# Normalising the mixer's output with tokens on partitions, and issuing the last sequence's tail in the second phase

## The reference, cut to what matters

```python
n  = layernorm(x) * (1 + scale_a) + shift_a
xs, z = split(n @ W_in.T)                 # 512 channels each
B, C  = xs @ W_B.T, xs @ W_C.T            # 16 states each
dt = softplus(xs @ W_dt.T + b_dt)
h[t] = exp(dt[t]*A) * h[t-1] + dt[t]*B[t]*xs[t]      # per channel and state
y[t] = sum_over_states(h[t]*C[t]) + D*xs[t]
x1 = x + gate_a * ((y * silu(z)) @ W_out.T)
h2 = layernorm(x1) * (1 + scale_b) + shift_b         # over the 256 features
out = x1 + gate_b * two_layers(h2)                   # attention (window 128), gated MLP
```

## Time and profile before

| what | us |
|---|---|
| three runs: median (lowest to highest) | 4182.83 (4182.79 to 4183.98) |
| the profiled execution | 4186.23 |
| its span, first to last instruction | 4184.4 |
| set-up and the first sequence's head, until the first x load of the loop after it | 0 to 55 |
| from the first to the last-but-one x1 store of phase one (14 passes) | 195.0 to 1646.2 |
| phase one's last store | 1751.0 |
| phase two: first store of layer 0, last store of layer 0 | 1953.2, 3037.7 |
| first and last store of the output | 3117.0, 4181.1 |

### The profile page before, as it was taken

One profiled execution on the slowest core, in us unless ns is written; L12 is line 12 of the kernel. 1 busy time (PEld: TensorE's weight loads), 2 busy tenths in 40 slices (PEclk: granted clock), 3 DMA queues, 4 the chain that ended last, 5 costly groups with the idle time before them and its releaser, 6 DMA issues.

```text
span 4184.4 us, 61077 instructions
## 1 busy us (share of the span) xinstructions
PE 3982.3 (95%) x19870; PEld 2670.8 (64%) x19870; DVE 3624.9 (87%) x6114; ACT 2743.5 (66%) x5896; POOL 2670.3 (64%) x1298
## 2 busy tenths in 40 slices
PE   7999999999999999769999999999999999999997
PEld 4444444444444444347887778787777878777785
DVE  5999999999999999768888888877888887878884
ACT  6677777777777775336767676666767666666764
POOL 3999999999999999553434444443534444343442
PEclk8999999999999999879999999999999999999998
DMA  3333333333333333420000000001110101000010
GB/s 109 117 124 124 122 122 121 122 121 121 122 122 123 125 122 116 137 91 27 21 26 17 31 16 31 16 31 51 36 63 21 41 21 37 26 31 32 21 36 26
DMA packets 119610, 295.11 MB, mean 71 GB/s; under 512 B 21288, under 2 KB 45664, under 8 KB 119296
## 3 DMA queue, kind: packets, MB, share of 16 engines
q1 hardware_dynamic: 117424, 291.15, 21.1%
q10 hardware_dynamic: 1872, 0.05, 0.0%
HBM read 248.52 MB, written 42.64 MB: 70 GB/s over the span
## 4 chain that ended last, share of the span: by engine, by line
PE 51%; DVE 2%; ACT 1%; DMA 1%; issue 1%; POOL 1%; SPq 0%; DVEq 0%; ACTq 0%; POOLq 0%
PE b_bank L1346 12%; PE b_bank L1474 12%; PE b_bank L1495 6%; PE b_bank L1425 5%; PE b_bank L1398 5%; PE b_bank L1409 5%; PE b_bank L1439 4%; PE b_bank L1378 3%; DMA b_hx<-stack_rows 1%; PE b_bank L1446 1%; ACT b_probs_t L1586 0%; DVE b_hx_part L1728 0%; DVE b_qk_rot L1773 0%; PE b_bank L1510 0%; POOL b_scores L1704 0%
## 5 line engine op out<-in xcount | busy, mean ns | idle before, releaser
L824 POOL TENSOR_TENSOR a_state<-a_state,a_c_wide 128x1024 f32<-128x1024 f32 x512 | 1195.1, 2371 | 19.7 <-DVE a_state L766 19.7
L1704 POOL TENSOR_TENSOR b_scores<-b_scores,b_row_rate 128x1024 f32<-128x1024 f32 (+1 forms) x256 | 458.2, 1801 | 825.6 <-DVE b_row_rate L1825 825.6
L584 PE MATMUL a_y_sum<-a_state,a_ident 128*128 128x512 f32 x2048 | 951.2, 597 | 6.8 <-POOL a_state L824 6.8
L766 DVE TENSOR_TENSOR_SCAN a_state<-a_decay,a_slot 128x1024 f32<-128x1024 f32 x352 | 788.7, 2270 | 0.7
L1346 PE MATMUL b_bank<-b_w_qkv,b_hx_part 128*128 128x512 f32 x2304 | 604.8, 408 | 29.9 <-DVE b_hx_part L1728 9.1
L584 PEld LDWEIGHTS a_y_sum<-a_state,a_ident 128*128 128x128 f32 x2048 | 387.3, 191 | 383.0 <-issue 316.7
L1677 POOL TENSOR_TENSOR b_by_cos<-b_qk,b_rotary 128x1024 f32<-128x1024 f32 x128 | 310.2, 2424 | 475.5 <-DVE b_qk L1757 473.4
L1474 PE MATMUL b_bank<-b_hn_part,b_w 128*128 128x512 f32 x2112 | 526.2, 399 | 7.0 <-DVE b_hn_part L1728 6.9
L695 ACT ACTIVATE a_decay<-a_dt,a_neg_a 128x512 f32<-128x512 f32 x704 | 453.8, 710 | 114.5 <-DVE a_state L766 114.1
L1574 ACT ACTIVATE b_scores<-b_scores,b_row_bias 128x256 f32<-128x256 f32 (+1 forms) x1024 | 478.2, 472 | 69.4 <-DVE b_row_bias L1814 69.4
L1346 PEld LDWEIGHTS b_bank<-b_w_qkv,b_hx_part 128*128 128x128 f32 x2304 | 428.3, 192 | 128.8 <-issue 16.4
(11 more groups left out here) (211 smaller groups left out, 6946.2 us busy)
## 6 DMA issues: line engine op xcount, KB each, us to landing
a_c_wide<-bc_rows SPq DMA_DIRECT2D x256, 512.0 KB, 3.8
a_b_wide<-bc_rows SPq DMA_DIRECT2D x80, 512.0 KB, 4.8
b_hx<-stack_rows SPq DMA_DIRECT2D x64, 256.0 KB, 3.9
b_x_res<-stack_rows SPq DMA_DIRECT2D x32, 512.0 KB, 3.4
a_xt<-in_L_attn_x SPq DMA_DIRECT2D x16, 512.0 KB, 5.4
x_rows<-a_x_t SPq DMA_DIRECT2D x16, 512.0 KB, 5.4
stack_rows<-a_h_t SPq DMA_DIRECT2D x16, 512.0 KB, 5.3
stack_rows<-b_xc SPq DMA_DIRECT2D x16, 512.0 KB, 2.9
```

The lines of the kernel that those rows point to most:

```text
L584: last = nc.tensor.matmul(y_sum[dd][:], ident[:], state[state_ring.slot[q]][:, i, :], start=False, stop=(j == GROUPS - 1 and i == GROUP - 1))
L766: nc.vector.tensor_tensor_scan(flat(h), flat(factor), flat(term), 0.0, ALU.mult, ALU.add).then_inc(scan_done.sem, 1)
L824: nc.gpsimd.tensor_tensor(h[:], h[:], c_wide[c_ring.slot[q // 2]][:], ALU.mult).then_inc(cmul_done.sem, 1)
L1704: nc.gpsimd.tensor_tensor(probs, probs, row_rate[:, w, at].unsqueeze(2).to_broadcast([P, 4, hi - lo]), ALU.mult)\
```

## The change: what it does

Seven things are changed together.

1. The tail's normalisation has tokens on partitions. `turn2` (PE, 8 transposes of x1), `tot2` (ACT copies 4 tiles of 128x256 out of PSUM with a row sum), `stat2` (ACT: mean, 4 squares with a row sum, Ln, Exp), `norm2` (ACT: 4 shifts of 128x1 and 4 scalings of 128x256), `hT2` (PE, 8 transposes back) and `h2` (ACT modulates from PSUM). `mean2`, `cen2`, `sq2`, `var2`, `dev2` and `xn2` go.
2. B and C go through the spreading matmul as two F32R parts on 64 rows. `bcrest` and `bcmid` go.
3. Unit 9's `mul` goes from POOL to DVE (`TO_VECTOR = 9`), with a `bcast` of its own.
4. The one-column cut of dt goes from POOL (L807) to ACT (`cut`).
5. The tail of sequence 15 leaves phase one: its steps are issued by each engine inside `FIRST_ORDER` of phase two, so phase one's block ends with the last gate. Banks 6 and 7 are free for phase two when its `h2` is done.
6. SP in phase two: `load_first` comes ahead of the first pass and holds layer 0's weights and the three early spares. The later spares, `w_o` and the vectors (`load_rest`) stay behind phase one's last stores, after `h2store:0` in the first pass. At the change of layer, the q and k weights are asked for as soon as the last projection that used them is done, and `w_1` and `w_2` two passes later in `load_hx`, after the rows.
7. `MIXER_ORDER`, `ORDER`, `BANK_OF` and `FIRST_ORDER` are all new. The head's `norm` writes in place and waits for the transposes of x, and sequence 0's `norm` moves from the set-up to the loop. In the set-up one load goes and `picks` is F32.

```diff
-    1: "xload xT xcopy stat norm hT mod up hcut xs xscopy bc bccopy cstore bcup bcrest bcmid bclow dt soft dtadd"
-       " z zcopy silu",
+    1: "xload xT xcopy stat norm hT mod up hcut xs xscopy bc bccopy cstore bcup bclow dt soft dtadd"
+       " z zcopy silu cut",
     0: "skip bcast cload bload decay mul scan cmul sum gate",
-    -1: "out res x1store mean2 cen2 sq2 var2 dev2 xn2 h2 h2store"}
+    -1: "out res x1store turn2 tot2 stat2 norm2 hT2 h2 h2store"}
+TAIL_STEPS = MIXER_STEPS[-1].split()
...
-        by_pool = [q for q in units if q // 2 in POOL_LOADS]
+        by_pool = [q for q in units if q // 2 in POOL_LOADS and q != TO_VECTOR]
...
-                    last = nc.tensor.matmul(slots[q % 2][:, i, :], picks[0:96, GROUP * j + i, :], bc_parts[slot][0:96, :],
+                    last = nc.tensor.matmul(slots[q % 2][:, i, :], picks[:, GROUP * j + i, :].bitcast(F32R), bc_parts[slot][:].bitcast(F32R),
                                             start=True, stop=True)
...
+            def copy_tail(s, slot, i):
+                wait(act, h2_turned, s - 1, CHUNKS)
+                wait(act, x1_turned, s, i + 1)
+                for t in (2 * i, 2 * i + 1):
+                    at = (t % 2) * DIM
+                    nc.scalar.activation(xn2[t], bank(f"turn2{i}")[:, at:at + DIM], ACT.Copy, accum_out=neg_mean2[:, t:t + 1])\
+                        .then_inc(total2_done.sem, 1)
...
 FIRST_ORDER = """
-pss:0 pnorm:0 prot:0 padd:0 pq:0 pk:0 v:0 pss:1 psq:0 prate:0 vc:0 psq:1 prate:1 ptc:0 pnorm:1 pk:1 prot:1 vc:1 vc:2
-psq:2 prate:2 v:1 pq:1 padd:1 hxs:0 pss:2 pnorm:2 v:2 ptr:0 prot:2 padd:2 pk:2 ptc:1 pq:2 psq:3 hxload:0 pq:3 pss:3
-pnorm:3 prot:3 ptr:1 padd:3 pk:3 ptc:2 prate:3 ptc:3 ptr:2 mask:0.0 mask:0.1
+out:0 pq:0 pk:0 res:0 psq:0 pss:0 prate:0 pnorm:0 out:1 v:0 res:1 x1store:0 vc:0 prot:0 turn2:0 turn2:1 tot2:0
+tot2:1 pk:1 pq:1 psq:1 padd:0 pss:1 prate:1 pnorm:1 v:1 stat2:0 vc:1 prot:1 padd:1 ptr:0 pq:2 pk:2 psq:2 pss:2 ptc:0
+v:2 prate:2 pnorm:2 norm2:0 vc:2 prot:2 ptr:1 padd:2 hT2:0 hT2:1 h2:0 h2:1 h2store:0 hxload:0 pk:3 pq:3 psq:3 pss:3
+ptc:1 prate:3 hxs:0 pnorm:3 ptr:2 ptc:2 v:3 vc:3 prot:3 padd:3 ptc:3 pn:0.0 pn:0.1
 """
...
                 if s == BATCH:
                     for done, group in zip(moved, (early, late)):
                         sp.wait_ge(done, 3 * loads_of(group))
-                    load_qkv()
+                    sp.wait_ge(q_full.sem, q_full.at(s - 1, TILES))
+                    load_qkv(0)
+                    sp.wait_ge(k_full.sem, k_full.at(s - 1, TILES))
+                    load_qkv(1)
+                    sp.wait_ge(v_done.sem, v_done.at(s))
+                    load_qkv(2)
```

More of the change, by code:

```diff
@@ L116, in host_constants @@
     pick = np.zeros((P, STATES), np.float32)
-    for part in range(3):
+    for part in range(2):
         pick[2 * STATES * part + np.arange(STATES), np.arange(STATES)] = 1.0
@@ L161 @@
[L161 to L165, removed]
@@ L497, in _ @@
                           "h2store": store_h2})
+            for signal, per_pass in ((xs_full, INNER_CHUNKS), (z_full, INNER_CHUNKS), (bc_full, 1), (dt_full, INNER_CHUNKS)):
+                wait(sp, signal, BATCH - 1, per_pass)
+            wait(sp, h2_stored, 0, 1)
+            first.load(sp)
+            first.tail["SP"] = {"x1store": store_x1, "h2store": store_h2}
         @block.tensor
@@ L718, in _ @@
-                           "bcmid": middle_bc, "decay": decays, "sq2": square_tail, "dev2": deviation_tail, "h2": modulate_tail})
+                           "xscopy": copy_x, "zcopy": copy_z, "silu": silu, "soft": softplus, "cut": cut, "bccopy": copy_bc, "bcup": upper_bc,
+                           "decay": decays, "tot2": copy_tail, "stat2": statistics_tail, "norm2": normalise_tail, "h2": modulate_tail})
+            first.tail["ACT"] = {"tot2": copy_tail, "stat2": statistics_tail, "norm2": normalise_tail, "h2": modulate_tail}
@@ L804, in add_parts @@
                     .then_inc(u_done.sem, 1)
-                wait(pool, u_done, s, half + 1)
-                nc.gpsimd.tensor_tensor(dt[slot][:, pair, 0:1], half_cut[:], half_cut[:], ALU.add).then_inc(dt_done.sem, 1)
             def scan_input(s, slot, q):
@@ L840 @@
 ORDER = """
-ptr-:3 v-:3 hxs:0 mask:1.0 vc-:3 mask:1.1 score:0.0 score:0.1 score:1.0 hxload:0 exp:0 rate:0 add:0 pss:0 score:1.1
-wo:0 psq:0 pk:0 x1load:0 pq:0 add:1 exp:1 rate:1 wo:1 v:0 pnorm:0 prate:0 v:1 pt:0.0 pn:0.0 pn:0.1 pt:0.1 vc:0 mean:0
-score:2.0 pt:1.0 cen:0 pn:1.0 mask:2.0 resload:0 pt:1.1 pn:1.1 store:0 sq:0 pt:1.2 pt:1.3 prot:0 psq:1 vc:1 pq:1 sqs:0
-pss:1 padd:0 xn:0 mask:2.1 pk:1 dev:0 v:2 prate:1 vc:2 var:0 ptc:0 hns:0 hn:0 pnorm:1 att:0 mask:3.0 score:2.1 onorm:0
-onorm:1 prot:1 rate:2 padd:1 gated:0 ptr:0 pn:2.0 gated:1 hl:0 pss:2 outstore:0 exp:2 mask:3.1 gelu:0 gelu:1 psq:2
@@ new lines @@
+exp:1 wo:0 pq:0 pk:0 mask:1.1 wo:1 pn:1.0 rate:0 add:0 pt:0.0 pss:0 prate:0 x1load:0 add:1 rate:1 v:0 pt:0.1 mask:2.0
+pnorm:0 pn:1.1 score:2.0 cen:0 score:2.1 mean:0 v:1 mask:2.1 prot:0 sq:0 pt:1.0 pk:1 psq:1 sqs:0 pt:1.1 resload:0 vc:0
+pq:1 pss:1 pt:1.2 padd:0 pnorm:1 dev:0 prate:1 vc:1 xn:0 outstore:0 ptc:0 v:2 pt:1.3 vc:2 onorm:0 hns:0 hn:0 var:0
+mask:3.0 pk:2 att:0 ptr:0 mask:3.1 prot:1 rate:2 pn:2.0 padd:1 pq:2 hl:0 score:3.0 gated:0 pn:2.1 score:3.1 exp:2
+gelu:0 psq:2 gated:1 hl:1 gelu:1 pss:2 onorm:1 hh:0 att:1 hh:1 gelu:2 ga:0 hl:2 gated:2 prate:2 ptc:1 ga:1 pnorm:2
@@ L851 @@
+pn:3.0 ga:2 prot:2 ptr:1 exp:3 rate:3 gated:3 hh:2 ga:3 pt:2.0 ga:4 pt:2.1 wd:0 gelu:3 hl:3 gated:4 pt:2.2 wd:1 ga:5
+gelu:4 hh:3 pq:3 hl:4 pk:3 gated:5 wd:2 ptr:2 padd:2 pss:3 hl:5 wd:3 pn:3.1 hh:4 gelu:5 psq:3 pnorm:3 ptc:2 pt:2.3
+wd:4 hh:5 store:0 fin:0 prate:3 pt:3.0 wd:5 fin:1 pt:3.1 sum:0 pt:3.2 prot:3 turnc:0 sum:1 padd:3 turnc:1 pt:3.3 vc:3
+ptc:3 pn+:0.0 v:3 att:2 turn:0 turn:1 pn+:0.1 onorm:2
 """
 BANK_OF = """
-q_t3:5 k_t3:1 wo0:5 s0_0_0:6 s0_0_1:0 s0_1_0:4 s0_1_1:5 wo1:7 s1_0_0:2 s1_0_1:3 q0:4 k0:1 s1_1_0:0 s1_1_1:6 pt0_0:3
```

332 lines of the change are left out of this document (172 added, 160 removed).

## The result

The changed kernel takes 4218.2 us (median of 4 runs, 4217.2 to 4218.9) against 4182.8 for the kernel before on the same chip: ratio 1.0085, 95% interval 1.0068 to 1.0103. It is 0.85% slower, where -44 us were forecast. Its profiled execution took 4217.7, with a span of 4215.8.

What follows compares the result with a forecast made beforehand. DVE was taken to bound phase one, PE phase two and a chain the seam. Terms -28 + 2 - 9 - 7.5 - 2 = -44.5 us gave 4141.7 from the profiled 4186.2, stated as 4139; own range 4124 to 4152, wider 4118 to 4166.

Steps and rivals of the forecast that it cites:

- Phase one, a pass: Phase one's passes: DVE binds and loses 1.72 us a pass, 103.66 to 101.94; PE needs 97.6 to 101.5; term -28.
- PE or ACT takes over: Rival for phase one: PE reaches 103.3 us a pass, the term is -8 in place of -28, 4159 us; chance 0.14.
- The first gate: Prologue: sequence 0's norm moves into the loop, a shorter cut of B and C offsets part; +2 us (0 to +6).
- The last pass: Last pass of phase one: has no head, is set by POOL with one mul fewer; -2 us.
- if the 0.34 of idle stay: Phase one: condition that DVE's idle 0.34 us a pass remains, for a pass to become 101.94.
- The clock: Phase one: by the skill's rule on transposes, PE's new 2.4 us could cost 2.4 more; weighed with the PE rival.
- The seam: Between phases: the block ends with the gate, 18.5 us sooner, but SP's queue gives back 10.2; taken as -9.
- the seam gives nearly all: Rival: h2 is early or the first attention pass gets shorter, 10 us more won, 4129 us; chance 0.13.
- The change of layer: Phase two's 80.20 us pass: q and k weights asked for earlier remove PE's wait behind queued loads; -7.5 us.
- the moved loads: Phase two: earlier q and k loads give -7.5 us, w_1 and w_2 no longer ahead of a rows load give -2.
- The rest of phase two: Other phase-two passes: PE is full, so the new order can't take much off 71.7; 0, bounds -0.3 and +2 a pass.
- the bound of -5 for phase one: Phase one's term of -28: its weak end, -5 us, if PE or ACT takes over.

Runs made afterwards that it cites:

- E6: The changed kernel with its F32R spreading matmuls on 96 rows instead of 64, the added rows zero; 4125.0 us.
- E4: The kernel before with only phase two's new ORDER, BANK_OF and FIRST_ORDER, without the tail's steps; 4134.3 us.
- E7: The kernel before with phase two's new order and also the moved loads of layer 1's weights; 4134.5 us.
- E11: The changed kernel with F32R spreading on 96 rows, and DVE's gates multiplying only 64 of 512 columns; 4112.2 us.

## Why the prediction was wrong

**The step that failed** is PE's price in "Phase one, a pass": "its spreading matmuls go from 44 at BF16 to 46 at F32R", put at -1.0 to +2.9 us. I priced the form from `dt`'s row of 128 rows and let the rows go from 96 to 64 without a term. The form was priced rightly for 96 rows: PE needs 100.3 a pass there, inside my 97.6 to 101.5. The rows cost 0.39 us a unit, 9 us a pass; with them PE is busy 106.7 of a pass of 109.2, and DVE waits for it. The rival "PE or ACT takes over" named the engine, but its upper end, 103.3, was built on the same price.

**Phase one's own gain** would have been missed too. E6 stands 4 us behind before at the last gate, not 26 ahead. The first gate comes 5 us later (131.7 against 126.6, where I said +2; E4 and E7, with before's own set-up, show 129.6 and 126.7, so 3 of the 5 can be scatter). DVE loses 1.0 of busy time a pass and not 1.7, a third of that is lost in waits among three engines, and 0.6 us a pass goes to the clock. The last pass, said to give 2, gave nothing. "if the 0.34 of idle stay" was the weak clause. POOL was taken as no bound once unit 9 had moved, and it is none (100.3 busy); without that move a pass would be 105.4.

**The clock.** The Trainium skill's page "TensorE: Matmul & The Clock Gate", part 4, says that transposes don't count as work that keeps the clock up; I weighed it as 2.4 us more a pass. After's five passes with 32 transposes each average 1.00, with one short fall among them (the windows show 0.82, 0.50 and 0.83 from 666 to 672 us), so that price is not seen. What the runs do show is a clock that falls at a stretch of waits, and holds when ordinary matmuls take the place of the waiting.

**The seam** held. After's queue of SP shows sequence 1's rows asked for at 1894.96, which is +68.0 from the last gate's end (1826.94), where +69.5 was counted; the spare stores come directly behind the loads, as said:

```profile
1868.26 0.34 SPq L507 DMA_DIRECT2D stack_rows<-a_h_t  x1
...
1884.64 1.62 SPq L1296 DMA_DIRECT2D b_w_whole<-in_L_ffn_w  x2
1886.30 5.69 SPq L1289 DMA_DIRECT2D w_part<-b_probs_t  x6
1892.03 2.88 SPq L1289 DMA_DIRECT2D w_part<-b_scores  x4
1894.96 1.09 SPq L1313 DMA_DIRECT2D b_hx<-stack_rows  x2
```

With phase two's order equal (E6 against E7), gate to first store is 202.7 against 214.1: -11.4 for -9. The other 7 us come with phase two's new order (before against E7), as the rival "the seam gives nearly all" had it. Together they are 19, over the 15 that was to count as wrong.

**The change of layer** was right in size and wrong in cause. The pass of 80.20 became 71.2, but E4 has 70.8 with the old loads; the moved loads, priced at -9.5 together, gave 0 within 3 us.

**The rest of phase two**, "taken at 0; bounds -0.3 and +2", was the second failure: "the new `ORDER` and `BANK_OF` can't take much off 71.7", since PE is full. Of the idle 0.25 that I had read the order took about 0.2 in E4, as the bound of -0.3 allowed. The rest came out of busy time: full meant busy, and busy time can hold the price of switches between row counts, which an order saves. That this is the rest is argued above and not shown. In all the order gave 0.95 us in each pass of layer 0 and some 1.3 in layer 1.

Two slips in the sums play no part: 4141.7 less 3.4 is 4138.3 and not 4139, and the bound of -5 for phase one should be the rival's -8.

## What to carry to other kernels

A matmul has a price to its neighbour, not only its own: read the start-to-start times at each change of contraction rows, and pad 64 rows to 65 or 96 with zeros when it stands among ones of 128. Count such switches before calling a full engine's stretch fixed. And where the granted clock dips behind a wait, try giving the engine work there, since taking work away can cost what it saves.

## What the runs showed of the hardware

- Between FP32 sums of 128 rows a spreading pair costs 0.39 us (F32R) or 0.27 us (BF16) more at 64 rows than at 96. At 65 rows the price is gone: 4125.1 us in place of 4218.2 for one added zero row.
- Six matmuls a pass whose values nobody reads (1.4 us) made the kernel 9.6 us faster, some 7 of them because the clock stayed at 1.00. One fall to 0.50 cost a pass 1.7 us.
- Why the array needs the longer hand-over at 64 rows, and what exactly lets the clock fall (E11's PE waits 1.77 us at the same place as E6's and falls once, not five times), stays open.
